# Decay exponents of a chunked scan: from TensorE outer products to broadcast running sums and GpSimd

## The reference, cut to what matters

```
dt     = softplus(A_log)                # one number per token and head
cum    = cumsum(-dt) within a chunk     # the running sum
decay  = exp(cum[q] - cum[k]) where q >= k, else 0      # 128 x 128 per head and chunk
y_intra = (C B^T * decay) x
states  = (B * exp(cum[last] - cum))^T x                # per chunk
y_inter = (C * exp(cum)) prev_state
```

## Time and profile before

| | us |
|---|---|
| median of 3 runs | 405.5 (405.41 to 407.51) |
| the profiled execution | 406.83 |
| its span, first to last instruction | 405.1 |
| busy, PE / DVE / ACT / POOL | 386.7 / 332.6 / 226.6 / 176.2 (95 / 82 / 56 / 43% of the span) |
| start of the first unit's decay (ACT L806) | 38.1 |
| first statistics after the scan (DVE L964) | 241.7 |

### The profile page before, as it was taken

How to read it: one execution, slowest core, us unless ns; L and a number is a source line. 1 busy time by engine, 2 the same in 40 slices (tenths; PEclk the granted TensorE clock), 3 DMA queues, 4 the chain that set the end, 5 groups by cost and what they waited for, 6 DMA issues and landing times.

```text
span 405.1 us, 8904 instructions
## 1 busy us (share of the span) xinstructions
PE 386.7 (95%) x3023; PEld 299.3 (74%) x3023; DVE 332.6 (82%) x564; ACT 226.6 (56%) x422; POOL 176.2 (43%) x208
## 2 busy tenths in 40 slices
PE   8998999999999999996989999899999999999996
PEld 8686676766766767764767777568888888888886
DVE  5988899999999999997989938738958759696685
ACT  6766556465565564568676632664554545546541
POOL 3699411101111101106456920235686665867661
PEclk9999999999999999999999999989999999999999
DMA  6311220322220122213411150000102020200003
GB/s 186 100 54 25 58 64 8 115 56 61 62 59 28 41 59 63 61 35 109 128 49 25 49 162 1 0 2 1 60 19 78 3 78 13 65 0 2 0 2 104
DMA packets 35932, 21.13 MB, mean 52 GB/s; under 512 B 17048, under 2 KB 33760, under 8 KB 35904
## 3 DMA queue, kind: packets, MB, share of 16 engines
q1 hardware_dynamic: 35904, 20.78, 18.3%
HBM read 18.13 MB, written 1.31 MB: 48 GB/s over the span
## 4 chain that ended last, share of the span: by engine, by line
PE 70%; DVE 13%; ACT 8%; issue 6%; POOL 2%; ACTq 0%; DVEq 0%; POOLq 0%
PE bank L1283 22%; PE bank L1259 10%; PE bank L1249 9%; PE bank L1478 8%; PE bank L1252 5%; PE bank L1398 3%; PE bank L1269 2%; PE bank L1466 2%; DVE conv L1228 2%; PE bank L1307 2%; PE bank L1425 2%; DVE conv L1021 2%; POOL el L656 1%; ACT conv L695 1%; PE bank L1486 1%
## 5 line engine op out<-in xcount | busy, mean ns | idle before, releaser
L1021 DVE SCALAR_TENSOR_TENSOR conv<-bank,taps,conv 128x510 f32<-128x510 f32 (+2 forms) x204 | 149.8, 745 | 17.4 <-ACT conv L695 12.3
L1283 PE MATMUL bank<-uth,parts 128*128 128x512 f32 x272 | 95.3, 407 | 1.1 <-DVE utl L1004 0.9
L695 ACT ACTIVATE conv<-bank,tap_b,taps 128x512 f32<-128x512 f32 x68 | 52.9, 777 | 69.6 <-PE bank L1283 58.9
L569 POOL TENSOR_TENSOR ce<-conv,ecx 128x512 f32<-128x512 f32 x15 | 19.4, 1291 | 117.5 <-DVE conv L1021 117.5
L1283 PEld LDWEIGHTS bank<-uth,parts 128*128 128x128 f32 x272 | 51.0, 187 | 18.9 <-issue 3.5
L651 POOL TENSOR_TENSOR ul<-conv,uh 128x512 fp32r<-128x512 f32 x32 | 42.9, 1357 | 40.5 <-ACT uh L922 27.5
L656 POOL TENSOR_TENSOR el<-conv,parts 128x512 fp32r<-128x512 f32 x30 | 44.3, 1504 | 30.3 <-ACT parts L934 30.3
L1283 PE MATMUL bank<-utl,parts 128*128 128x512 f32 x136 | 53.5, 393 | 0.0
L1216 DVE CAST uh<-conv 128x512 fp32r<-128x512 f32 x28 | 26.0, 966 | 22.5 <-ACT conv L918 21.9
L1228 DVE TENSOR_TENSOR conv<-conv 128x512 f32<-128x512 f32 x32 | 31.4, 1014 | 11.9 <-ACT conv L939 11.8
L1106 DVE SCALAR_TENSOR_TENSOR g<-dec,bank 128x512 f32<-128x512 f32 x64 | 40.8, 678 | 0.0
(11 more groups left out here) (208 smaller groups left out, 743.3 us busy)
## 6 DMA issues: line engine op xcount, KB each, us to landing
w_raw<-in_L_attn_W_in_dram SPq DMA_DIRECT2D x17, 256.0 KB, 3.2
ecx<-ecum_dram SPq DMA_DIRECT2D x32, 128.0 KB, 2.9
ew_raw<-in_L_ffn_Wup_dram SPq DMA_DIRECT2D x7, 256.0 KB, 2.9
ew_raw<-in_L_ffn_Wgate_dram SPq DMA_DIRECT2D x7, 256.0 KB, 3.1
ew_raw<-in_L_ffn_Wdown_dram SPq DMA_DIRECT2D x7, 256.0 KB, 3.8
xres<-in_x_dram SPq DMA_DIRECT2D x2, 512.0 KB, 4.2
out_dram<-xres SPq DMA_DIRECT2D x4, 256.0 KB, 2.1
yi<-yev SPq DMA_DIRECT2D x56, 16.0 KB, 1.8
```

What stands on the lines that cost most here:

```text
L695: act.activation(conv[q][:, j, HALF * h:HALF * (h + 1)], bank[u % 2][:], ACT.Identity, bias=tap_b[q][:, j:j + 1], scale=taps[q][:, j, TAPS ...
L1021: dve.scalar_tensor_tensor(out=dst[:, :, d:SEQ], in0=src[:, :, 0:SEQ - d], scalar=taps[q][:, j, TAPS - 1 - d:TAPS - d], in1=dst[:, :, d:SE ...
L1283: ins = pe.matmul(bank[u % 2][:], w, x_t, start=(i == 0), stop=(i == 3 * KD - 1))
```

## The change

The exponent of a unit is no longer made on PE. `cum_dram` now holds the running sums in f32. For each unit a DMA copies the 2 KB of its four chunks to all 128 partitions (`cumb`, 256 KB), POOL writes -1e30 where the later token is not later (`mask`, affine_select) and adds the negated sum of the partition's own token (`spans`; from `ncp`, a copy of `ncum`, which PE transposes and ACT negates once). ACT takes the exponential of `cumb`. `cumb` has one buffer per unit, so the load for the next pair waits for the exponential of this one.

SP's order in a pair is now: the second half of `cumb` for pair n, `place_y(n-1)`, `ecx`, `w`, `taps`, and then the first half of `cumb` for pair n+1. In the last pair POOL masks all four units and then adds all four, before anything else.

On PE the four exponent groups of a pair go, and `turn_w` moves to where exponents 0 and 1 were (the state then uses bank 4). DVE makes the taps of two units crossed (`crossed_taps`): (v,1) (v,2) (v+1,1) (v,3) (v+1,2) (v+1,3), and the waits for taps are counted by `taps_by`. Extra work of the late pairs is spread over more pairs (`over_pairs` writes out four more). The constants, the splitting of the sums and the fills of `cr` are gone.

```diff
-            def load_cum(m, q):
-                at_least(sp, expo_done, 4 * (m - 2))
...
+            def load_cumb(m, h):
+                at_least(sp, exp_done, 4 * (m - 2) + 2 * h + 2)
+                for j in range(2):
+                    row = T * (2 * (m - 1) + j) + T // 2 * h
+                    sp.dma_start(cumb[2 * h + j][:],
+                                 cum_dram[row:row + T // 2, :].partition_broadcast(P)).then_inc(cumb_in[h], 16)
...
-                if n < PAIRS:
-                    load_cum(n + 1, 1 - q)
+                if n > 1:
+                    load_cumb(n, 1)
                 if 1 < n < PAIRS:
                     sp.wait_ge(y_read, n - 1)
                     place_y(n - 1, 1 - q, yev_out[1 - q])
...
                 if n + 2 <= PAIRS:
                     load_taps(n + 2, q)
+                if n < PAIRS:
+                    load_cumb(n + 1, 0)
...
+            def mask(u):
+                pool.affine_select(out=cumb[u][:], in_=cumb[u][:], compare_op=ALU.is_ge, fill=NEG, base=0,
+                                   pattern=[[0, T // 2], [1, P]], channel_multiplier=-1).then_inc(masked, 1)
+            def spans(n, q, u):
+                pool.wait_ge(masked, 4 * (n - 1) + u + 1)
+                h, j = u // 2, u % 2
+                from_s = ncp[q][:, j, 2 * h:2 * h + 2, :].rearrange("p b c -> p (b c)").unsqueeze(2).to_broadcast([P, T // 2, P])
+                pool.tensor_tensor(cumb[u][:], cumb[u][:], from_s, ALU.add).then_inc(span_done, 1)
...
             def body(n, k, q):
                 end = isinstance(n, int) and n == PAIRS
+                pool.wait_ge(cumb_in[0], 32 * n)
+                pool.wait_ge(ncp_done, n)
                 if end:
+                    pool.wait_ge(cumb_in[1], 32 * n)
+                    for u in range(4):
+                        mask(u)
+                    for u in range(4):
+                        spans(n, q, u)
                     decay_c_half(n, q, 0)
...
+                at_least(pool, stT_done, n - 1)
+                copy_xs(n + 1, 1 - q)
+                mask(0)
+                mask(1)
+                spans(n, q, 0)
+                spans(n, q, 1)
+                at_least(pool, y_done, 4 * (n - 1))
+                copy_x(n + 1, 1 - q)
+                decay_c(n, k, q)
+                pool.wait_ge(cumb_in[1], 32 * n)
+                at_least(pool, exp_done, 4 * (n - 1))
+                copy_ncum(n + 1, 1 - q)
+                mask(2)
+                mask(3)
+                spans(n, q, 2)
+                spans(n, q, 3)
...
             def decays(n, u):
-                a, b = 4 * (n - 1) + u, u % 2
-                act.wait_ge(expo_done, a + 1)
-                at_least(act, g_done, a - 1)
-                act.activation(dec[b][:], bank[4 + b][:], ACT.Exp).then_inc(exp_done, 1)
+                a = 4 * (n - 1) + u
+                act.wait_ge(span_done, 4 * (n - 1) + u + 1)
+                at_least(act, g_done, a - 3)
+                act.activation(dec[u][:], cumb[u][:].rearrange("p i t -> p (i t)"), ACT.Exp).then_inc(exp_done, 1)
...
+            def crossed_taps(m, q, v):
+                done = 12 * m + 3 * v
+                for i, (u, d) in enumerate(((v, 1), (v, 2), (v + 1, 1), (v, 3), (v + 1, 2), (v + 1, 3))):
...
+                    if d == 1:
+                        dve.wait_ge(acc_first, 4 * m + u + 1)
+                    else:
+                        dve.wait_ge(tap_done, done + (0, 1, 0, 2, 3, 5)[i])
...
                 turn_state(n - 1)
                 weigh(n - 1, 1 - q, 2)
-                exponents(n, k, q, 0)
-                exponents(n, k, q, 1)
+                if not last(n, 2):
+                    turn_w(n + 2, k + 1, q, lambda: None)
                 from_state(n - 1, 0)
                 from_state(n - 1, 1)
                 weigh(n - 1, 1 - q, 3)
```

More of the change, by code:

```diff
@@ L103, in decoder_layer @@
         cum = sb("cum", [P, 2 * P])
-        crest = sb("crest", [P, 2 * P])
-        cparts = sb("cparts", [P, 3, 2 * P], BF16)
+        ncum = sb("ncum", [P, 2, P])
+        ncp = [sb(f"ncp{i}", [P, 2, NSEQ, 2]) for i in range(2)]
         ecum = sb("ecum", [P, P])
@@ L204, in decoder_layer @@
         taps_in = [sem(f"taps_in{i}") for i in range(2)]
-        cum_in = [sem(f"cum_in{i}") for i in range(2)]
+        cumb_in = [sem(f"cumb_in{i}") for i in range(2)]
         ew_in = [sem(f"ew_in{i}") for i in range(2)]
@@ L259, in over_pairs @@
             body(1, 0, 1)
-            with eng.Fori(1, PAIRS // 2 - 2) as k:
+            with eng.Fori(1, PAIRS // 2 - 4) as k:
                 body(2 * k, k, 0)
                 body(2 * k + 1, k, 1)
-            for n in range(PAIRS - 4, PAIRS + 1):
+            for n in range(PAIRS - 8, PAIRS + 1):
                 body(n, n // 2, n % 2)
@@ L268, in last, with taps_by @@
             return isinstance(n, int) and n + ahead > PAIRS
+        def taps_by(m, u):
+            in_turn = isinstance(m, int) and m < 2
+            return 12 * m + ((3, 6, 9, 12) if in_turn else (4, 6, 10, 12))[u]
         def over_experts(eng, body):
@@ L286, in y_bank, with st_bank @@
             return bank[6] if isinstance(n, int) and n == PAIRS and h else bank[7]
+        def st_bank(n):
+            return bank[6] if isinstance(n, int) and n == PAIRS else bank[4]
         def up_bank(e, v):
@@ L612, in body @@
+                spans(n, q, 2)
+                spans(n, q, 3)
+                if not isinstance(n, int):
+                    return
+                if n == 1:
+                    weigh_context()
+                if n in (PAIRS - 7, PAIRS - 6):
+                    for v in range(2 * (n - PAIRS + 7), 2 * (n - PAIRS + 7) + 2):
                         pool.wait_ge(zgate_done, v + 1)
                         pool.tensor_tensor(z_part(v), z_part(v), zgate(v), ALU.mult).then_inc(z_gated, 1)
-                    if isinstance(n, int) and n in (PAIRS - 3, PAIRS - 2) and u == 3:
-                        pool.wait_ge(z_gated, 4)
-                        gate_y(0, n - PAIRS + 3)
@@ L630, in body @@
[L630 to L639 removed]
+                if n in (PAIRS - 5, PAIRS - 4):
+                    pool.wait_ge(z_gated, 4)
+                    gate_y(0, n - PAIRS + 5)
@@ L870, in body @@
                 copy_state_turned(n)
+                if not first:
+                    act.wait_ge(ce_done, n - 1)
                 beside(n, m, km, r, 2)
```

217 lines of the change are left out of this document (78 added, 139 removed).

## The result

| | time, us | ratio to before |
|---|---|---|
| before | 405.75 median of 4 (405.41 to 407.51) | |
| after | 456.03 median of 4 (455.25 to 457.01) | 1.123, 95% interval 1.119 to 1.127 |
| forecast | 440 (424 to 460), slower with 0.92 | 1.085 |

Slower, as forecast and inside the range, but by 50 us where 34.5 were expected. The profiled execution spans 454.9 us; before it was 405.1.

A forecast was written before the change was run, and what follows sets the result against it. PE with DVE close behind bounded the kernel at 12.45 us a pair; afterwards a loop through SP, POOL and ACT would take 14.75. Span 405.1 + 24.9 (first pair, twelve periods) + 9.9 (last pairs) = 439.9; forecast 440 (424 to 460).

The forecast's parts named there:

- first pair: Start of the scan: the first `yev` copy ends at 54.4 us against 51.28 before, +3.1.
- twelve periods: `yev` copies 2 to 13 of the scan: 12 x 14.75 us, ending at 231.4 against 206.54 before.
- last pairs: From the 13th `yev` copy to the first statistics, by SP's order: 45.0 us against 35.1 before, +9.9.
- what follows: Everything behind the first statistics: unchanged, with 0 taken for a loss of PE clock and up to 3 us allowed.
- The loop: Steady pairs: `yev` copy, SP's line, `cumb` landing, POOL, ACT's exponentials, next `yev` copy; period 14.75 us, 2.3 more than before.
- line of SP: Loop term: SP's unbroken issues of `place_y`, `ecx`, `w` and `taps` before the first `cumb` half, 6.03 us.
- landing: Loop term: two `cumb` DMAs of 256 KB issued 0.63 apart, the second landing 3.1 to 3.2 after its issue: 3.7 us.
- from the state's part to the first statistics 4.6: End of the last pair: once POOL has made the C part, 4.6 us remain until the first statistics.
- The loop of PE and DVE: Steady pairs: C B^T, taps, g and C B^T again together allow a period of 11.9 us, 0.55 less than before.
- Rival 1: POOL and DMA at their high bounds: the same loop at 16.9 us, time 471; chance 0.15.
- Rival 2: PE's relief wins, not slower: first `cumb` half reaches POOL in time, loop under 11.9 us, time 400; chance 0.09.
- Rival 3: GpSimd slows DVE: ten taps and g longer by 0.6 us, DVE loop 17.9, time 478; chance 0.02.

The follow-up runs named there:

- e1: Kernel after the change, with SP issuing the first half of the next pair's `cumb` right behind `ecx`, ahead of `w` and `taps`: 432.0 us.
- e4: Kernel after the change without POOL's masks, the exponential's argument scaled by 0.01, so the result is not the layer's: 439.1 us.
- e2: Kernel after the change, with SP issuing the first half of the next pair's `cumb` before `place_y`: 426.5 us.
- e3: As e2, with pair 16's second `cumb` half ahead of the second `load_late`, and GpSimd masking and adding by halves in pair 16: 416.9 us.
- e5: As e3, with SP issuing the store of the 1024 context sums behind the broadcasts of its iteration, the `sig` loads one iteration later: 416.7 us.
- e9: As e6, with the store of the 1024 sums issued by ScalarE on its own queue in pair 8, `sig` loads in iteration 9: 418.9 us.
- e8: Kernel after the change, with 26 added matmuls into a free bank in the last pair, ahead of the first product with x: 454.65 us.
- e11: Kernel before the change, with ScalarE's side work of pairs 12 to 15 ahead of the first taps of units 0 and 2: 403.1 us.
- e12: As e9, with ScalarE's late side work ahead of first taps, and GpSimd gating the second y group's second half behind pair 16's masks, spans and `ce`: 411.5 us.
- e6: As e5, with the second half of pair 15's broadcast issued ahead of the twelve late loads: 418.4 us.

## Why the prediction was right, and where it was short

The predicted span was 439.9, the measured one 454.9. The 15.0 lie so:

| step of the prediction | predicted | measured | missed by |
|---|---|---|---|
| first pair, end of `yev` 1 | 54.4 | 53.05 | -1.35 |
| twelve periods | 177.0 | 189.4 | +12.4 |
| last pairs, `yev` 13 to statistics | 45.0 | 50.5 | +5.5 |
| what follows ("unchanged") | 163.4 | 161.9 | -1.5 |

**The loop: right, 14.75 predicted, 15.16 measured.** By terms, with the measured one second: line of SP 6.03 and 6.02 (116.39 to 122.41); landing 3.7 and 4.40 (122.41 to 126.81); POOL with its wake 4.05 and 3.57 (to 130.38 by its last span's end), less since a span is 1.02 from start to start, not 1.25; ACT 0.95 and 1.14 (to 131.52), the two exponentials not in one block as the span of the second comes 1.0 behind the first. So the sum fits better than its terms: GpSimd was priced 0.5 too high and the landing 0.7 too low. The second `cumb` landed 3.9 after its own issue, where the prediction took 3.1 to 3.2. Four `cumb` go out back to back here, and the prediction counted two; that this is the reason isn't shown, since where only two went out (248.01 and 262.24) the second took 4.4 and 3.6. e1 and e4 each shorten one term, e2 takes the `yev` wait out of it, and all three periods fit the same loop.

**Twelve equal periods: short by 7.5.** Periods 2, 9 and 10 are 17.3. The step said that extra work in the slack is hidden, and of ACT's and DVE's work that held (period 7, with the table load, is 15.1, where e2 and e3 show 15.0 without the slow loop). What it left out is that the terms of the loop itself, SP's issues and the landing, vary with the rest of the traffic. Period 2 is long by one stall of SP's queue, 10.7 us behind the store of the sums; two `ecx` issues take 1.23 elsewhere:

```profile
71.48 3.17 SPq L325 DMA_DIRECT2D ecx<-ecum_dram  x2
```

That is 1.9 of the 2.1. It is not the 6 to 7 us that the store costs in e3, e5 and e9, where a load that is waited for stands behind it, and it doesn't come every time: in e8, whose kernel is the same up to the last pair, these two issues took 1.23 and period 2 is 15.10.

In periods 9 and 10 SP's line took 7.37 and 7.36 for 6.02, and the second `cumb` landed 4.8 and 5.0 after its issue for 3.9. The landing has the expert weights beside it, three loads of 256 KB issued just behind the first half. The line of period 9 does not: its long issues come before those loads, and what made them long is open.

```profile
180.88 1.12 SPq L303 DMA_DIRECT2D w_raw<-in_L_attn_W_in_dram  x1
182.56 1.75 SPq L310 DMA_DIRECT2D tap_b<-in_L_attn_conv_b_dram  x2
184.35 0.91 SPq L317 DMA_DIRECT2D cumb<-cum_dram  x2
185.30 0.43 SPq L382 DMA_DIRECT2D ew_raw<-in_L_ffn_Wup_dram  x1
```

In e1 the expert weights go out 3 us behind the first half; its landing is 4.1 there, and periods 9 and 10 (13.18 and 13.52) are like the others. No run takes the weights out.

**Last pairs: short by 5.5.** GpSimd's masks began 34.8 us behind the end of `yev` 13 where 32.3 was reckoned (+2.5, SP's line and landing). Masks and spans were 1.0 shorter. The step that failed is "from the state's part to the first statistics 4.6": that piece is 4.57 (288.41 to 292.98), but PE does not start it when the C part is there, at 284.4. Ahead of it in PE's order stand a product with x, the new state, two projections, a transpose and C B^T, 5.5 us that wait for the `yev` copy of pair 15, and that copy for the exponentials behind GpSimd:

```profile
282.90 0.63 PE L1410 MATMUL bank<-g,xp 128*16 128x128 f32 x8 [8.00 <-ACT yev L789]
283.30 0.66 PE L1419 MATMUL bank<-btok,xs 128*32 128x128 f32 x8
283.88 1.22 PE L1450 MATMUL bank<-xres,ident 128*128 128x256 f32 x2
284.90 1.91 PE L1456 MATMUL bank<-woT,yi 128*128 128x256 f32 x4
286.61 0.42 PE L1425 MATMUL bank<-ident,stT 128*128 128x128 f32 x1
286.96 1.52 PE L1477 MATMUL bank<-conv 64*128 64x128 f32 x16
288.41 0.29 PE L1437 MATMUL bank<-ce,state 128*16 128x128 f32 x2
```

That is +4.0. The prediction took the state's part as the head of the stage without reading what is queued ahead of it. At full clock two such projections take 0.70 and 1.03 (288.96, 289.49) for 1.22 and 1.91, so by an estimate from these rows about 2 us of the 5.5 are the clock's, which the prediction took as 0 and allowed up to 3.

**What follows: 1.5 shorter.** e11, whose kernel behind the scan is that of before, also takes 161.9 there. So the 1.5 probably belong to the one profiled execution of the kernel before, 163.4, and not to the change.

**Single operations.** Mask: 0.60 taken, 0.61 from start to start (0.637 alone). Span: 1.25 taken, 1.02 measured. Six crossed taps: 4.24 taken, 4.18 measured. The loop of PE and DVE: 11.9 taken, 12.07 measured.

```profile
L499 POOL TENSOR_TENSOR cumb<-cumb,ncp 128x512 f32<-128x512 f32 x64 | 65.2, 1040 | 0.0
L491 POOL TENSOR_SCALAR_AFFINE_SELECT cumb<-cumb 128x512 f32<-128x512 f32 x64 | 39.2, 637 | 6.7 <-DMA cumb<-cum_dram 6.7
```

**The rivals.** Rival 1 (high bounds) fell with the mask at 0.64; that the time, 456, lies near its 460 is by other terms. The range's upper end was drawn from a dear mask, and that the result still lies inside it is luck. Rival 2 (relief wins) decides below 11.9; e2 and e3 make that case with one moved call, and it is worth 0.4 us a pair. Rival 3: with GpSimd busy 58% of the span, six crossed taps take 4.18 from start to the next operation, less than the 4.45 in turn of the earlier trace rows, and single ones 0.74 as there (in the earlier trace rows the longest is 749 ns, not 748).

**What the change costs at its best.** e12 and e11 have the same order of side work. Their spans, cut at the same `yev` copies: to `yev` 2, 65.67 and 64.79 (+0.9); five periods to 7, 60.3 and 62.4 (-2.0); period 7 with the store of the sums, and the old kernel's plain one, 21.1 and 12.4 (+8.6); to `yev` 14, 77.9 and 76.8 (+1.0); to the statistics 22.6 and 23.0 (-0.5); the rest +0.3. Sum +8.3, of 409.6 and 401.3. PE's relief is there, 0.4 us a pair, and one stretch outweighs it. It holds the small store, with loads behind it that PE and GpSimd wait for; the DMA engines' share around it is 0.44, where e11 has 0.22:

```profile
65.67:126.00 60.33, 57.12 (x565) 42.66 (x565) 56.64 (x86) 35.80 (x71) 42.35 (x67) 1.00 0.44 137
126.00:147.06 21.06, 12.77 (x115) 9.41 (x117) 12.69 (x19) 10.88 (x20) 8.39 (x15) 0.83 0.68 79
```

The 8.6 are not the store's alone. In e12 period 7 also holds ScalarE's table load and gates, which e11 has in period 11 (13.93). With them and without the store, period 7 of e6 is 15.0. So the store's part lies between 6.1 and 9.0 (a plain period is 12.1), and without it e12 would, by an estimate from these numbers, span 400.6 to 403.5, about where e11 stands with 401.3. Whether there is a place for the store with 14 us of nothing urgent behind it was not tried.

## What to carry to other kernels

When work moves from a busy engine to a free one, draw the loop of its new inputs and outputs through every queue that they pass, and add it up: here the "free" GpSimd path had a period of 15.2 us against 12.45, and one moved DMA call was worth 30 us. Then list everything else that uses the loop's resources, even once, since a loop without slack pays for each. At the end of a stage, read what is queued ahead of its first instruction on that engine, and not only what that instruction waits for.

## What the runs showed of the hardware

- Loads of 256 KB issued up to 5.5 us behind a store of 1024 single 4-byte values (4 KB in all) landed after 9.8 to 14.1 us instead of 3.2 to 3.6, on its own queue (e3, e5) and on the other one (e9).
- Issues of `cumb` took 0.47 us each back to back, where `yev` and `ecx` take 0.6; behind the 1024 values four issues of `place_y` took 7.4 in e3 and 5.1 in the kernel before, for 2.6.
- Four broadcasts of 256 KB issued back to back: the second landed 4.4 us after the issue of the first.
- A GpSimd addition of 128x512 with the second input broadcast along its rows took 1040 ns, against 1290 with two full inputs; a mask (affine_select) of 128x512 took 637.
